# Selective scan in double blocks: 2080-column scans, a carry in four pieces, a loop round of twelve sequences

## The reference, cut to what matters

```python
def step(hst, ins):
    dt_t, B_t, C_t, x_t = ins
    dA = jnp.exp(dt_t[:, :, None] * A)
    hst = hst * dA + (dt_t * x_t)[:, :, None] * B_t[:, None, :]
    y_t = jnp.einsum('bds,bs->bd', hst, C_t)
    return (hst, y_t)
_, ys = jax.lax.scan(step, h0, (tm(dt), tm(Bm), tm(Cm), tm(xs)))
```

## Time and profile before

| what | value |
|---|---|
| median of 3 runs | 8310.11 us (8305.58 to 8311.34) |
| the profiled execution | 8306.97 us |
| its span, first to last instruction | 8305.2 us |
| the scans, first start to last end | 978.0 to 5729.3 us |
| DVE, ACT, PE, POOL busy in the whole span | 76%, 72%, 87%, 16% |
| mean granted clock of TensorE | 0.923 |

### The profile page before, as it was taken

How to read it: one execution, slowest core, us unless ns; L and a number is a source line. 1 busy time by engine, 2 the same in 40 slices (tenths; PEclk the granted TensorE clock), 3 DMA queues, 4 the chain that set the end, 5 groups by cost and what they waited for, 6 DMA issues and landing times. The chain is left out here.

```text
span 8305.2 us, 233928 instructions
## 1 busy us (share of the span) xinstructions
PE 7213.0 (87%) x94400; PEld 3879.0 (47%) x94400; DVE 6337.9 (76%) x5597; ACT 5946.5 (72%) x8090; POOL 1364.6 (16%) x799
## 2 busy tenths in 40 slices
PE   7999588888888888888888888887989999989998
PEld 5444344444444444444444444444444444445554
DVE  2555599999999999999999999997444544546554
ACT  2555599999999999999999999995233544445554
POOL 0000132222222222222232322231000000000000
PEclk9999798999988888999999988898999999999999
DMA  4666422222222222222222222223510000000000
GB/s 151 154 148 143 112 68 65 66 65 63 65 66 66 63 66 67 66 66 63 67 66 66 66 62 65 65 69 131 182 44 8 9 8 8 3 31 11 9 11 6
DMA packets 621179, 542.24 MB, mean 65 GB/s; under 512 B 490224, under 2 KB 528752, under 8 KB 606448
## 3 DMA queue, kind: packets, MB, share of 16 engines
q1 hardware_dynamic: 620032, 526.35, 21.8%
HBM read 380.72 MB, written 145.49 MB: 63 GB/s over the span
## 5 line engine op out<-in xcount | busy, mean ns | idle before, releaser
L1266 DVE TENSOR_TENSOR_SCAN s_h<-s_decay,s_h 128x1040 f32<-128x1040 f32 x2048 | 4618.2, 2323 | 166.8 <-ACT s_decay L1190 162.8
L1161 ACT COPY s_h<-s_pb 128x1024 f32<-128x1024 f32 x2048 | 2516.3, 1229 | 232.0 <-PE s_pb L1092 205.1
L1105 PE MATMUL s_py<-s_h,s_cz 128*32 128x128 f32 x32768 | 2516.7, 437 | 1.9 <-DVE s_h L1266 1.9
L1190 ACT ACTIVATE s_decay<-s_pa 128x1024 f32<-128x1024 f32 x2048 | 2177.2, 1063 | 56.8 <-issue 44.4
L1077 PE MATMUL s_pa<-s_dl,s_al 18*128 18x64 bf16 x32768 | 912.7, 198 | 705.4 <-ACT s_decay L1190 564.2
L1105 PEld LDWEIGHTS s_py<-s_h,s_cz 128*32 128x32 f32 x32768 | 1057.3, 126 | 460.5 <-issue 4.7
L1077 PEld LDWEIGHTS s_pa<-s_dl,s_al 18*128 18x128 bf16 x32768 | 662.8, 98 | 1029.5 <-ACT s_decay L1190 907.7
L1092 PEld LDWEIGHTS s_pb<-s_ul,s_bl 18*128 18x128 bf16 x16384 | 494.5, 97 | 1071.3 <-ACT s_h L1161 859.1
L1092 PE MATMUL s_pb<-s_ul,s_bl 18*128 18x128 bf16 x16384 | 870.9, 229 | 70.4 <-issue 54.4
L1233 POOL TENSOR_TENSOR s_h<-s_h,s_one 128x64 f32<-128x64 f32 x384 | 715.2, 1863 | 723.5 <-DVE s_h L1266 723.5
L1221 POOL TENSOR_TENSOR s_cz<-s_cl,s_one 128x128 f32<-128x128 f32 x256 | 318.8, 1245 | 2762.1 <-PE s_py L1105 2750.4
(11 more groups left out here) (218 smaller groups left out, 5977.0 us busy)
## 6 DMA issues: line engine op xcount, KB each, us to landing
s_bl<-B SPq DMA_DIRECT2D x1024, 72.0 KB
s_ul<-U SPq DMA_DIRECT2D x1024, 72.0 KB
s_dl<-D SPq DMA_DIRECT2D x1024, 72.0 KB
s_al<-A SPq DMA_DIRECT2D x256, 144.0 KB
D<-p_dp SPq DMA_DIRECT2D x64, 384.0 KB, 6.5
U<-p_up SPq DMA_DIRECT2D x64, 384.0 KB, 5.6
B<-p_bz SPq DMA_DIRECT2D x144, 128.0 KB, 2.2
SZ<-p_sz SPq DMA_DIRECT2D x16, 1024.0 KB, 5.1
```

Source lines behind the costliest of these rows:

```text
L1105: mm = pe.matmul(py[e % 2][QR * q:QR * q + QR, 0:P], cz[e % 2][:, l * P + QR * q:l * P + QR * q + QR], states, start=(l == 0), stop=(l == ...
L1161: act.copy(out, pb[:].rearrange("p b t d -> p d b t")).then_inc(bu_done, 1)
L1190: act.activation(decay[(STEPS * e + 2 * z + j) % RING][:, :, 1:W], pa[j % 2][:], ACT.Exp).then_inc(exp_done, 1)
L1266: dve.tensor_tensor_scan(seg, decay[(STEPS * e + 2 * z + j) % RING][:].rearrange("p d w -> p (d w)"), seg, 0.0, ALU.mult, ALU.add).then_in ...
```

## The change

A scan now covers two steps (32 channels, 32 x 65 = 2080 columns). STRIDE = 2 steps make one scan, HALVES = 4 scans make a block, and `scanned` counts these. The `decay` ring has 3 buffers of twice the size, in place of 6; ACT still fills them 1024 columns at a time, each time in one half of a buffer. The carry is written in four pieces of 32 channels, each after one scan of the block before. `take_y` stands ahead of the exponential of step 7. The loop has 5 rounds of 12 sequences, so that there are 4 jumps.

```diff
-    RING = 6
+    STRIDE = 2
+    HALVES = STEPS // STRIDE
+    RING = 3
     HB = 3
 ...
     BEHIND = 6
+    ROUND = 4 * HB
 ...
-        decay = [sb(f"decay{e}", [P, FG, W]) for e in range(RING)]
+        decay = [sb(f"decay{e}", [P, STRIDE * FG, W]) for e in range(RING)]
 ...
             body(0, True, False, 0)
-            with eng.Fori(0, (SEQS - 1) // HB - 1) as g:
-                for q in range(HB):
-                    body(HB * g + (1 + q), False, False, (1 + q) % HB)
+            with eng.Fori(0, (SEQS - 1 - HB) // ROUND) as g:
+                for q in range(ROUND):
+                    body(ROUND * g + (1 + q), False, False, (1 + q) % HB)
 ...
-                        wait(pe, scanned, STEPS * (k + 1))
+                        wait(pe, scanned, HALVES * (k + 1))
 ...
-                            if j == BEHIND and not (first and e < 2):
+                            if j == BEHIND + 1 and not (first and e < 2):
                                 take_y(k - 2, e)
 ...
-                            wait(act, scanned, STEPS * k + j + 1 - RING)
-                            act.activation(decay[(STEPS * e + 2 * z + j) % RING][:, :, 1:W], pa[j % 2][:], ACT.Exp
+                            at = j // STRIDE
+                            wait(act, scanned, HALVES * k + at + 1 - RING)
+                            part = slice(FG * (j % STRIDE), FG * (j % STRIDE + 1))
+                            act.activation(decay[(z + e + at) % RING][:, part, 1:W], pa[j % 2][:], ACT.Exp
                                            ).then_inc(exp_done, 1)
 ...
-                    for g in range(2):
-                        rows = slice(P // 2 * g, P // 2 * (g + 1))
+                    for g in range(HALVES):
+                        rows = slice(STRIDE * FG * g, STRIDE * FG * (g + 1))
                         if e:
-                            wait(pool, scanned, STEPS * (k - 1) + STEPS // 2 * (g + 1))
+                            wait(pool, scanned, HALVES * (k - 1) + g + 1)
 ...
-                        for j in range(STEPS):
-                            if j % (STEPS // 2) == 0:
-                                wait(dve, carried, 2 * k + j // (STEPS // 2) + 1)
-                            wait(dve, exp_done, STEPS * k + j + 1)
-                            seg = hb[to][:, FG * j:FG * j + FG, :].rearrange("p d w -> p (d w)")
-                            dve.tensor_tensor_scan(seg, decay[(STEPS * e + 2 * z + j) % RING][:].rearrange("p d w -> p (d w)"),
+                        for j in range(HALVES):
+                            wait(dve, carried, HALVES * k + j + 1)
+                            wait(dve, exp_done, STEPS * k + STRIDE * (j + 1))
+                            rows = slice(STRIDE * FG * j, STRIDE * FG * (j + 1))
+                            seg = hb[to][:, rows, :].rearrange("p d w -> p (d w)")
+                            dve.tensor_tensor_scan(seg, decay[(z + e + j) % RING][:].rearrange("p d w -> p (d w)"),
                                                    seg, 0.0, ALU.mult, ALU.add).then_inc(scanned, 1)
```

More of the change, by code:

```diff
@@ L1228, in carry @@
                     to, before = (z + e) % HB, (z + e - 1) % HB
-                    for g in range(2):
-                        rows = slice(P // 2 * g, P // 2 * (g + 1))
+                    for g in range(HALVES):
+                        rows = slice(STRIDE * FG * g, STRIDE * FG * (g + 1))
                         if e:
-                            wait(pool, scanned, STEPS * (k - 1) + STEPS // 2 * (g + 1))
+                            wait(pool, scanned, HALVES * (k - 1) + g + 1)
                             pool.tensor_tensor(hb[to][:, rows, 0], hb[before][:, rows, TB],
-                                               one[:].to_broadcast([P, P // 2]), ALU.mult).then_inc(carried, 1)
+                                               one[:].to_broadcast([P, STRIDE * FG]), ALU.mult).then_inc(carried, 1)
                         else:
-                            wait(pool, scanned, STEPS * (k - HB + 1))
+                            wait(pool, scanned, HALVES * (k - HB + 1))
                             pool.tensor_tensor(hb[to][:, rows, 0], zcol[:, rows],
-                                               one[:].to_broadcast([P, P // 2]), ALU.mult).then_inc(carried, 1)
+                                               one[:].to_broadcast([P, STRIDE * FG]), ALU.mult).then_inc(carried, 1)
                 def sequence(n, first, last, z):
```

## The result

The changed kernel takes 8165.83 us (median of 4 runs, 8164.36 to 8168.2), the kernel before in the same runs 8307.85 (8304.43 to 8311.34): a ratio of 0.9829, 95% interval 0.9812 to 0.9846. That is 142 us faster, where 62 were forecast. The direction was right; the size was not. The time lies in the stated range (8160 to 8330), 6 us above its lower end, and outside its likely part (8210 to 8295).

The account below looks back on a forecast made before the run. DVE's scans set the pace, with ACT just ahead. Changes of -61 fixed parts, -75 jumps, -38 short waits, +107 POOL and +5 ends gave -62 us: 8248 us, range 8160 to 8330, likely 8210 to 8295.

Parts of the forecast that it names:

- one operation per scan end: POOL is shut out while a DVE scan runs; only one POOL operation gets in each time a scan ends.
- one wait of DVE for POOL per block: At each block's first scan DVE waits for carry piece 0; piece 1 enters the same pause; 0.45 us a block.
- ACT with a lead up to the ring's length: With the output copy one step later, ACT's block takes 17.6 us, not 18.11, so it gets ahead of DVE.
- the coarser ring: Three double-size `decay` buffers leave ACT 4.5 us of slack, so waiting for whole double scans was costed at nothing.
- the slower rival: DVE gets the ports before piece 1, then waits for POOL at every scan: 410 us toll, 8469 us; chance 0.15.
- the race: After DVE's pause for piece 0, whether POOL's piece 1 or DVE asks first; POOL estimated ahead by 0.17 us.
- POOL's toll: Delay of DVE by carry pieces, fill and wait: 0.74 us a block, 189 us in place of 82.
- Jumps: Loop jumps where ACT stands still and DVE idles: 5.0 us each, 19 become 4, leaving 20 us, removing 75.
- The 38 us that I gave to the output copy: DVE's short waits, mostly at step 6 where ACT waits for PE, end with the copy at step 7: -38 us.
- Fixed part of a scan: 0.06 of each DVE scan's 2.215 us does not go by columns and falls away 1024 times: -61 us.
- The stage's two ends: First scan starts one exponential and copy later, last scan is twice as long: 2 us each, +5 us.
- no debt: Rival: POOL gets in without making DVE wait; toll 108 us, stage 4608, time 8167 us; chance 0.13.

Follow-up runs that it names:

- memset experiment: Changed kernel with a POOL memset of 512 columns of an unused tile behind each of a carry's first three pieces: 8360.03 us, ratio 1.0063 to the kernel before.

## Why the prediction was right in kind and wrong in size

What held: the exclusion between POOL and DVE, one operation per scan end, five operations for four ends, one wait of DVE for POOL per block (236 seen, "about 250" forecast), at the block's first scan, with piece 1 in the same pause; all the gain in the scan stage; ACT with a lead up to the ring's length; the coarser ring at next to no cost (0.8 us of waits for ACT behind the first scan). The memset experiment shows that the slower rival was a real one and that it hung on the race.

What failed is the sum. The stage was forecast 62 us shorter and is 141 shorter. Term by term:

- **POOL's toll**, forecast 189 us, measured 4610.0 - 4487 = 123, or 0.48 a block in place of 0.74. This is the step that was mis-sized most, 66 of the missing 79 us. The rows of one block give the same: it takes 18.02 us (3157.64 to 3175.66), 0.49 more than four clean starts. I put the wait at 0.45, the fill at 0.16 and the other two pieces at 0.065 each. The start behind the pause comes 4.81 after the one before (3152.83 to 3157.64), 0.43 late: 0.17 are the fill's (a scan of 4.63 for a clean one of 4.46), and 0.26 are the wait. The other three starts are 0.06 late together, the two pieces some 0.02 each. Of the wait, DVE's return was near (0.12 after the piece's end against 0.13 forecast, of which 0.05 stood on no row); but the piece, half as large as a carry before, reached only 0.14 past the point at which DVE would have started, not 0.20; and piece 1 did not hold DVE up by 0.10. The scan behind the pause takes 4.49, as long as behind a pause in the memset run in which no piece reaches into the scan (a piece ends at 3156.03, the scan starts at 3156.15).
- **Jumps**, forecast 20 us for the 4 that are left, measured 0.4 of waiting at one of them, and 1.7 in all the stage's waits that are not for POOL. I had allowed for a lead, and not taken it. Here the reasoning was wrong and not only a number: I gave 75 us to the longer rounds. The runs show that with the output copy moved, 19 jumps cost no more than 4 (double scans, 8166.52 and 8165.83). The two parts do the same work: alone they bring 86 and 127 us, and behind the second the first adds nothing. The 38 us that I gave to the output copy were a third of what it brings by itself.
- **Fixed part of a scan**, forecast 0.06 us, measured 2 x 2.215 - 4.382 = 0.05: 50 us and not 61.
- **The stage's two ends**, forecast 5 us. No run isolates them. The first scan starts 1.3 us later (979.3 against 978.0), and what the last one adds is inside what I call the toll.

As misses: 66 + 20 - 11 + 5 = 80. As changes: -95 for all 19 jumps, -38 for the short waits, -50 fixed parts, +41 POOL (123 in place of 82), gives -142, and 141.3 were measured. This sum had to close, as the toll is what is left over; the check of it is the 0.49 of the rows. And that it closes does not make its terms worth their size one by one. Given the output copy, the double scans with their five POOL operations and the longer ring buffers bring 9 us (8175.94 to 8166.52, both with rounds of three; 13 in the stage): 50 of fixed parts against the additional toll. The double scans without the output copy give nothing (8303.59).

The rival "no debt" gave 8167, and the time was 8166; but its mechanism is not what happened, since DVE waits for POOL 236 times. It stood at the right place for the wrong reason. The forecast's own terms reached down to 8190 only; the range went on to 8160 because of this rival. So it is luck that the time fell inside. No debt is what two pieces give: 8132.58, for which that rival's own toll of 108, reckoned for four pieces, would be 19 too high.

Why does a piece of 32 channels cost DVE 0.02 us at a scan's end, one of 64 about 0.09 and the fill of 128 elements 0.17? I had scaled by elements. The rows say something simpler. Each reaches past the start of the next scan, and that scan gets longer by the reach less 0.11 to 0.12 us:

| scan | POOL operation ahead | reaches in by | scan longer by |
|---|---|---|---|
| 3154.11 before | carry of 64, until 3154.31 | 0.20 | 2.38 - 2.29 = 0.09 |
| 3152.83 after | fill, until 3153.11 | 0.28 | 4.63 - 4.46 = 0.17 |
| 3162.05 after | piece of 32, until 3162.19 | 0.14 | 4.48 - 4.46 = 0.02 |

The medians over the stage, where DVE does not pause, are like them: 0.21 and 0.09 for 298 carries before, 0.28 and 0.17 for 254 fills and 0.14 and 0.02 for 396 pieces after; the zero pieces leave 0.13 (0.19 and 0.05 for 100 before). By this, piece 1, which reached in by 0.10, should cost nothing, and the 4.49 fits that. Open is why the last 0.11 to 0.13 us of a POOL row cost DVE nothing; no run isolates it.

## What to carry to other kernels

Where two engines have the same pace and neither has work queued, look for the small wait on the one that feeds: taking out half a microsecond of it per block brought 127 us, as the wait had kept the buffer between them empty and so let every stall through. Terms that remove the same stall don't add up; try each alone and both together before one is called the gain. If two engines exclude each other by instruction, count the operations of the one per end of an instruction of the other, before making instructions longer or the pieces smaller; and see whether a third engine with time left can take one.

## What the runs showed of the hardware

- A POOL operation with SBUF inputs that asks after DVE's start (0.05 us after it at 3157.69, 0.40 in the memset run) is shut out for the whole scan, at 2080 columns as at 1040 (medians of 4.45 and 2.27 us), and at 4160 too (8.86 in one case). The Trainium skill (SBUF — State Buffer, "Who interferes with whom") says that only a GpSimd operation that reads SBUF contends with such a VectorE one. The memset only writes, and it agrees: it took 514 to 557 ns in all 768 cases. 754 of these run on into a scan, by 0.32 at 3156.15, and this scan, at 4.49, is no longer than one behind a pause of the changed kernel. Six begin 0.07 to 0.08 us after a scan's start, where a piece would be shut out, as this one after a start at 986.25:

```profile
986.33 0.52 POOL L1248 MEMSET s_spare<- 128x512 f32 x1
```

- By the Trainium skill (SBUF — State Buffer, "SBUF: two separate sides") the one that starts first has the ports for its whole instruction. For DVE's side the rows agree. For POOL's side they agree but for the last 0.11 to 0.13 us of its row, as the table above shows. Piece 1 in the pause, which reached 0.10 us into a scan, cannot decide it.
- The granted clock of TensorE was 0.90 in the scan stage before and 0.95 after (means over its two levels, 1.2 GHz = 0.5 and 2.4 GHz = 1, so mostly the upper), with the same matmuls in 141 us less. No run here tells whether it had a part in the gain. Over the whole span it was 0.92 before, 0.95 after and with the output copy alone, 0.93 with rounds of twelve alone or the copy back at step 6, and 0.93 in the memset run, the slowest of all.
